# Three attention phases of a decoder: heads' values taken for two chunks in a row, and a new opening

## The chip, the cores and the metric

The kernel runs on one NeuronCore of a Trainium2 chip. The metric is the device time of one execution in microseconds (us), lower is better. Times are given as the median of several executions; the profile comes from one execution of its own.

## The reference

Two transformer layers on x of 16 batches (B), 256 tokens (S) and 512 features (C), with 16 heads of width 32:

```python
x = layer0_cross_attention(x, ctx, mask) + x      # pre-LN of x and ctx, softmax over 256 keys, output projection
x = x + fc2(gelu(fc1(LN(x))))
x = layer1_self_attention(x)                      # causal, LN after it
x = layer1_cross_attention(x, ctx)                # LN, relu feed forward, LN
```

Each attention computes q and k·v from features (512 wide products), scores q·k per head, a softmax over the keys, and the weighted sum of the values. A key row that is entirely zero is handled in layer 1 by a length ("energies" of one query against all keys decide where a row is cut). All is float32; a product is made of three passes on rounded parts (hi·hi, lo·hi, hi·lo), whose rounded halves are named `_hi` and `_lo`.

## The kernel before, in words

The program runs four phases after one another: **mask** (layer 0 cross attention), an MLP phase, **causal** (layer 1 self attention) and **cross** (layer 1 cross attention and feed forward). The change touches mask, causal and cross. They share `attention_phase`, with one program for each engine (SyncE, GpSimd = POOL, ScalarE = ACT, VectorE = DVE, TensorE = PE). A phase loops over the 16 batches. The heads of a batch are taken in four chunks (c = 0 to 3) of four heads. The order in which each engine issues its steps is written out by hand in `mask_turn`, `causal_turn` and `cross_turn`, for each engine its own; semaphores tie the engines together. Nothing reorders an engine's instructions: what stands behind a waiting instruction waits too. "Steady" batches are 1 to 15 in the loop; the first and last of a phase overlap the neighbouring phase or have no neighbour.

What happens to chunk c of batch b, by engine and line:

- `queries(b, c)` and `keys(b, c)` on PE (12 matmuls each, 256 columns, L172): q and k of four heads into one PSUM bank. ACT `qk` (L838 to 847) copies them rounded, DVE `qk_lo` (L1366 to 1371) makes the low halves. In causal and cross, POOL `query0` (L652) picks out a query, PE `energies0` (L2021) takes its product with all keys, and DVE `cuts` (L1374 to 1384) counts the kept keys (`flags`, L1379, signals `len_ready`) and writes the cut.
- `scores(b, c)` on PE (L2039, 24 matmuls on tiles of 32 rows by 128 columns; L2045 adds the cut).
- DVE minima (L1406 to 1412), then ACT `exps(b, u)` (L865, eight units' halves: u counts the heads, 4c to 4c+3), each followed by a read of its sum.
- `turn_probs(b, u)` on PE (L2060, four transposes, three in causal); ACT `copy(b, u)` (L877) takes them to `probT`.
- `attend(b, c)` on PE (L2079, 16 matmuls on tiles of 128 rows by 32 columns) into the left half of bank O; ACT `attended` (L885, L887) copies it to `OT`; PE `attended` (L2088, two transposes) turns it into the right half of O; DVE `attended` (L1432 to 1436: reciprocal, product, z) or, in mask, `turn_sums` (L2096, two transposes of the sums on PE) and DVE `normed` finish it. `attend` of chunk c stands behind `scores` of chunk c+1 (chunk 3 behind chunk 0 of the next batch).
- Between these steps PE does the `values` (L172), in mask `project`, in cross `feed1`, `feed2` and `post_turn`.

Order on PE around one chunk of the mask loop:

```python
turn_sums(b, 0)
scores(b, 1)
attend(b, 0)
queries(b, 2); keys(b, 2)
turn_probs(b, 4); turn_probs(b, 5); turn_probs(b, 6)
project(b, 0, 0); project(b, 0, 1)
turn_probs(b, 7)
```

The opening of the program: SyncE issues the loads of x and ctx of batch 0 (L391, L393), then `load_vecs` (L457 to 463; `where_vecs` L358 gives 16 small strided copies of the four layer norm vectors into `wcol`, columns of feature scales), then the weight matrices (L455), the mask (L443) and the rest. Then ACT `matrix_hi` (L815 to 818), DVE `matrix_lo` (L1264 to 1267) and `turned` (ACT L821 to 828; DVE L1351 to 1359, which for batch 0 also makes the high halves, L1357) prepare the first products; ACT normalizes x in L1197 ahead of them.

## Time and profile before

| | |
|---|---|
| median of 3 runs | 2745.2 us (2743.96 to 2746.96) |
| profiled execution | 2744.09 us, span 2742.4 us |
| granted TensorE clock | 0.995 of full speed |
| PE busy | 2672.3 us, 97% |
| DVE, ACT, POOL busy | 71%, 57%, 27% |
| mask phase, a steady batch | 39.31 us |
| causal phase, a steady batch | 33.25 us |
| cross phase, a steady batch | 49.27 us |

The span is the time from the first to the last recorded instruction; the execution's own time is 1.7 us longer. "PE busy" counts matmuls that overlap each other, so a small idle share doesn't mean that the engine works at its best rate. A steady batch is taken from the start of its first scores to that of the next batch's.

### The profile page before, as it was taken

The numbers are of one execution on the slowest core, as the hardware profiler recorded it, in microseconds if no ns is written. First come the engines' busy times: TensorE is split into PE (matmuls) and PEld (weight loads), VectorE is DVE, ScalarE is ACT, GpSimd is POOL, SyncE is SP. The second block draws the span as 40 slices with busy tenths as digits, with TensorE's granted clock in tenths as the row PEclk, the third lists the DMA queues.
The fourth block names the chain that finished last, engine by engine and source line by source line (L and its number), as shares of the span: only waits on it lengthen the run. The fifth ranks groups of instructions, "written<-read, shape, count | busy, mean of one in ns | idle before, by whom it ended". The sixth has DMA issues, their size and how long they took to land.

```text
span 2742.4 us, 68931 instructions
## 1 busy us (share of the span) xinstructions
PE 2672.3 (97%) x24032; PEld 2329.0 (85%) x24032; DVE 1952.7 (71%) x5572; ACT 1558.8 (57%) x4829; POOL 734.9 (27%) x935
## 2 busy tenths in 40 slices
PE   5999999999999999999999999999899999999997
PEld 5888888888888888888889999998788888888886
DVE  6878888887534443445388887887688888888876
ACT  5777777777211111111277777777676766767763
POOL 2333333330000000001013333333233434334343
PEclk9999999999999999999999999999999999999998
DMA  4333333342311211113021111112322212222110
GB/s 152 110 106 97 108 124 102 100 143 86 92 59 34 61 46 46 46 46 100 24 78 46 46 46 46 48 53 73 108 67 69 87 61 75 78 66 95 61 52 19
DMA packets 182230, 202.57 MB, mean 74 GB/s; under 512 B 19344, under 2 KB 109456, under 8 KB 181264
## 3 DMA queue, kind: packets, MB, share of 16 engines
q1 hardware_dynamic: 182160, 201.66, 23.3%
q8 instruction: 41, 0.67, 0.1%
q14 instruction: 29, 0.24, 0.0%
HBM read 137.65 MB, written 63.96 MB: 74 GB/s over the span
## 4 chain that ended last, share of the span: by engine, by line
PE 82%; DVE 8%; ACT 5%; issue 3%; POOL 1%; DMA 1%; SPq 1%; DVEq 0%; ACTq 0%; POOLq 0%
PE mask_work L172 13%; PE mlp_f L3028 13%; PE mlp_acc L3046 13%; PE causal_work L172 9%; PE cross_work L172 9%; PE mask_attended L2079 2%; PE mask_scores L2039 2%; PE mask_probsT L2060 2%; PE mask_scores L2060 2%; PE causal_scores L2039 2%; ACT cross_prob L865 2%; PE cross_probsT L2060 2%; PE causal_attended L2079 2%; PE cross_scores L2039 2%; PE causal_probsT L2060 1%
## 5 line engine op out<-in xcount | busy, mean ns | idle before, releaser
L2824 ACT ACTIVATE mlp_h<-mlp_f,mlp_b1col 128x512 f32<-128x512 f32 x128 | 88.3, 690 | 524.3 <-PE mlp_f L3028 524.3
L3028 PE MATMUL mlp_f<-mlp_xT_hi,mlp_w 128*128 128x512 f32 x1024 | 335.4, 389 | 0.0
L2929 DVE CAST mlp_hT_hi<-mlp_h 128x512 fp32r<-128x512 f32 x128 | 58.2, 454 | 369.8 <-ACT mlp_h L2824 369.7
L3046 PE MATMUL mlp_acc<-mlp_w,mlp_hT_hi 128*128 128x512 f32 x1024 | 315.2, 389 | 0.0
L865 ACT ACTIVATE mask_prob<-mask_scores,mask_low 128x256 f32<-128x256 f32 x512 | 237.7, 485 | 93.5 <-DVE mask_low L1412 93.4
L865 ACT ACTIVATE causal_prob<-causal_scores,causal_low 128x128 f32<-128x128 f32 (+1 forms) x512 | 211.0, 432 | 87.6 <-DVE causal_low L1412 87.6
L865 ACT ACTIVATE cross_prob<-cross_scores,cross_low 128x256 f32<-128x256 f32 x512 | 237.4, 497 | 33.2 <-DVE cross_low L1406 26.1
L1412 DVE CUSTOM_DVE_ANT_0 mask_scores<-mask_scores,mask_mask 128x256 f32<-128x256 f32 x512 | 198.9, 461 | 50.9 <-PE mask_scores L2039 50.3
L3028 PEld LDWEIGHTS mlp_f<-mlp_xT_hi,mlp_w 128*128 128x128 f32 x1024 | 192.1, 188 | 40.6 <-DVE mlp_xT_lo L2915 0.4
L3046 PEld LDWEIGHTS mlp_acc<-mlp_w,mlp_hT_hi 128*128 128x128 f32 x1024 | 192.2, 188 | 39.8
L172 PE MATMUL causal_work<-causal_xT_hi,causal_w 128*128 128x256 f32 x1008 | 221.8, 293 | 1.1 <-DVE causal_qk_parts L1371 1.1
L3028 PE MATMUL mlp_f<-mlp_xT_lo,mlp_w 128*128 128x512 f32 x512 | 199.2, 389 | 0.0
L3046 PE MATMUL mlp_acc<-mlp_w,mlp_hT_lo 128*128 128x512 f32 x512 | 199.2, 389 | 0.0
L1412 DVE CUSTOM_DVE_ANT_0 causal_scores<-causal_scores,causal_tri 128x128 f32<-128x128 f32 (+1 forms) x512 | 164.5, 394 | 25.3 <-PE causal_scores L2045 24.0
L172 PEld LDWEIGHTS causal_work<-causal_xT_hi,causal_w 128*128 128x128 f32 x1008 | 168.6, 189 | 13.2 <-issue 11.7
L652 POOL TENSOR_SCALAR causal_q<-all_own_head,causal_qk_parts 128x128 fp32r<-128x128 f32 x128 | 52.7, 423 | 431.7 <-DVE causal_qk_parts L1371 421.0
L1406 DVE TENSOR_REDUCE cross_low<-cross_scores 128x2 f32<-128x512 f32 x256 | 159.9, 681 | 5.0 <-issue 3.4
L652 POOL TENSOR_SCALAR cross_q<-all_own_head,cross_qk_parts 128x128 fp32r<-128x128 f32 x128 | 60.2, 482 | 369.3 <-DVE cross_qk_parts L1371 356.0
L2790 POOL TENSOR_TENSOR mlp_y<-mlp_x,mlp_b2r 128x512 f32<-128x512 f32 x32 | 45.3, 1447 | 398.5 <-DVE all_rows_largest L2945 363.5
L172 PE MATMUL causal_work<-causal_xT_lo,causal_w 128*128 128x256 f32 x504 | 142.0, 282 | 0.0
L877 ACT ACTIVATE mask_probT<-mask_probsT 128x512 f32<-128x512 f32 x128 | 80.6, 630 | 75.1 <-PE mask_probsT L2060 75.1
L865 ACT ACTIVATION_READ_ACCUMULATOR cross_prob<-cross_scores,cross_low 128x1 f32 x512 | 117.7, 230 | 0.0
(349 smaller groups left out, 8236.2 us busy)
## 6 DMA issues: line engine op xcount, KB each, us to landing
cross_x_in<-after_attention SPq DMA_DIRECT2D x17, 512.0 KB, 4.1
mask_x_in<-in_x SPq DMA_DIRECT2D x16, 512.0 KB, 4.5
mask_c_in<-in_ctx SPq DMA_DIRECT2D x16, 512.0 KB, 5.3
mask_res<-in_x SPq DMA_DIRECT2D x16, 512.0 KB, 3.7
after_attention<-mask_res SPq DMA_DIRECT2D x16, 512.0 KB, 2.8
mlp_x<-after_attention SPq DMA_DIRECT2D x8, 1024.0 KB, 5.5
mlp_stage<-in_L_xattn_fc_w SPq DMA_DIRECT2D x8, 1024.0 KB, 5.6
after_layer<-mlp_y SPq DMA_DIRECT2D x8, 1024.0 KB, 4.3
```

Of the source, the lines that this page charges most:

```text
L172: last = pe.matmul(out, lhs(k, a), rhs(k, c), start=(k == 0 and n == 0), stop=(k == KC - 1 and n == len(PASSES) - 1))
L652: ins = pool.tensor_scalar(Q0[:, part, :], own_head[:], QK[:, c % 2, 1 - part, 0:1].bitcast(F32), 1.0, ALU.mult, ALU.mult)
L865: ins = act.activation(prob[:, u % 4, qt, 0:w], SC[h][:, FROM[qt]:FROM[qt] + w], ACT.Exp, bias=low[:, u % 4, qt:qt + 1], scale=-1.0, accum ...
L877: act.activation(probT[:, u % 8, 0:n], PT_BANK[u % HC][:, 0:n], ACT.Copy).then_inc(s["copied"], 1)
L1406: ins = dve.tensor_reduce(low[:, u % 4, :], SC[h][:].rearrange("p (t k) -> p t k", t=TT), AX_X, ALU.min)
L1412: ins = dve.tensor_tensor_reduce(SC[h][:, at], SC[h][:, at], extra, 1.0, F32_MAX, ALU.add, ALU.min, low[:, u % 4, qt:qt + 1])
L2039: ins = pe.matmul(SC[h][:, at], QK[own, r, 1 - a, qt * P:(qt + 1) * P], QK[own, r, 2 + p, 0:WIDTH[qt]], start=(m == 0), stop=(masked_ctx a ...
L2060: ins = pe.transpose(PT_BANK[h][:, at:at + P], prob[:, u % 4, qt, kt * P:(kt + 1) * P], ident[:])
L2079: ins = pe.matmul(O[h * DH:(h + 1) * DH, q0:S], V[:, kt, HC * (c % KC) + h, :], probT[:, (HC * c + h) % 8, kt * S:kt * S + S - q0], start= ...
L2824: act.activation(h32[:, m % 2, :], F1[m % 2][:], ACT.Gelu, bias=b1col[:, m:m + 1]).then_inc(s["gelu"], 1)
L3028: ins = pe.matmul(F1[m % 2][:], W[2 * (m // 4)][:, a, k, m % 4 * P:(m % 4 + 1) * P], xT[p][:, k, :], start=(k == 0 and n == 0), stop=(k == ...
L3046: ins = pe.matmul(ACC[t][:], hT[a][:, m % 2, t * P:(t + 1) * P], W[2 * (m // 4) + 1][:, p, m % 4, :], start=(m == 0 and n == 0), stop=(m = ...
```

## The change

All three attention phases now take the values of two chunks in a row. `attend(b, 0, 2)` stands behind `scores(b, 2)` and `attend(b, -2, 2)` behind `scores(b, 0)` of the next batch (in cross the first of them stands after the first half of `feed1(b, 0)`, ahead of `turn_probs(b, 8)`), so chunks 1 and 3 hold no `attend`. Bank O holds both chunks, and the transposes overwrite it in place. `OT`, `sums`, `rs` and `rs32` are doubled; ACT copies both chunks back to back (one copy in mask), DVE's steps run once for a pair on 512 columns, `turn_sums` once with four transposes. `flags` is dropped: its step writes into `cut`.

The opening of mask takes the layer norm vectors as they lie, with four contiguous copies (`wraw`), and 16 matmuls by slices of the identity and one DVE copy make `wcol`. The third matrix is loaded ahead of the mask; the matrix halves and turned parts are done in another order; the high halves of batch 0 go from DVE to POOL.

Further moves: in cross, `turn_probs(b, -1)` comes ahead of `scores(b, 0)`, `turn_probs(b, 3)` and `turn_probs(b, 11)` ahead of the scores behind them, `queries(b+1, 1)` ahead of `energies0(b+1, 0)`, and ACT's copies 11, 14 and 2 ahead of `relu`, `qk` and `values`. In causal, `energies0` of chunks 2 and 0 come ahead of `turn_probs(b, 4)` and `turn_probs(b, 12)`. In mask, `keys(b+1, 0)` comes ahead of `turn_probs(b, 12)`.

```diff
     def where_vecs():
         if masked_ctx:
-            return [(wcol[q * QUAD:(q + 1) * QUAD, i, :],
-                     v.rearrange("(i k) q -> i k q", i=QUAD)[:, :, q:q + 1].rearrange("i k o -> i (k o)"))
-                    for i, v in enumerate(vecs[0:4]) for q in range(QUADS)]
+            return [(wraw[:, i, :], v) for i, v in enumerate(vecs[0:4])]
...
             load_vecs()
             load_matrix(0)
             load_matrix(1)
+            load_matrix(2)
             load_mask(0, first=True)
-            load_matrix(2)
...
+            for k in range(NP):
+                turned_hi(0, k)
             constants()
...
-            matrix_hi(0)
-            act.wait_ge(s["vec_loaded"], IT * NV)
+            matrix_hi(0, (0, 1))
+            act.wait_ge(s["columns_ready"], 1)
             turned(0, 0)
             turned(0, 1)
-            matrix_hi(1)
+            matrix_hi(0, (2, 3))
             turned(0, 2)
             turned(0, 3)
+            matrix_hi(1)
...
+            pe.wait_ge(s["vec_loaded"], IT * NV)
+            for k in range(KC):
+                for q in range(QUADS):
+                    ins = pe.matmul(PT[q * QUAD:(q + 1) * QUAD, 4 * k:4 * k + 4],
+                                    ident[:].rearrange("p (i k) -> p k i", k=KC)[:, k], wraw[:, :, q],
+                                    start=True, stop=True)
+            ins.then_inc(s["columns_ps"], 1)
...
-        def attend(b, c):
-
-            pe.wait_ge(s["copied"], UNITS * b + HC * (c + 1))
-            if c in (0, 2):
-                pe.wait_ge(s["v_ready"], 2 * b + 1 + c // 2)
+        def attend(b, c, n=1):
+
             pe.wait_ge(s["z_done"], KC * b + c + 1)
...
+            for c in range(c, c + n):
+                pe.wait_ge(s["copied"], UNITS * b + HC * (c + 1))
+                if c % 2 == 0:
+                    pe.wait_ge(s["v_ready"], 2 * b + 1 + c // 2)
+                at = S * (c % 2)
+                for kt in range(TT):
+                    q0 = P if causal and kt else 0
+                    for h in range(HC):
+                        ins = pe.matmul(O[h * DH:(h + 1) * DH, at + q0:at + S], V[:, kt, HC * (c % KC) + h, :],
+                                        probT[:, (HC * c + h) % 8, kt * S:kt * S + S - q0],
+                                        start=(kt == 0), stop=(kt == 1))
+                ins.then_inc(s["av_done"], 1)
+
+        def attended(b, c, n=1):
+
+            pe.wait_ge(s["ot_done"], KC * b + c + n)
+            for i in range(n):
+                for qt in range(TT):
+                    at = S * (c % 2) + (n * qt + i) * P
+                    ins = pe.transpose(O[:, at:at + P], OT[(c + i) % 2][:, qt * P:(qt + 1) * P], ident[:])
+            ins.then_inc(s["z_ps"], n)
```

The orders on PE, one phase each:

```diff
         def mask_turn(b, prev, cur, nxt):
...
-            turn_sums(b, 0)
             scores(b, 1)
-            attend(b, 0)
             pe.wait_ge(s["qk_lo"], KC * b + 2)
             queries(b, 2)
             keys(b, 2)
...
-            turn_sums(b, 1)
             if not nxt:
                 yield ROOM
             scores(b, 2)
-            attend(b, 1)
+            attend(b, 0, 2)
...
             turn_probs(b, 9)
+            turn_sums(b, 0)
...
         def causal_turn(b, prev, cur, nxt):
...
             scores(b, 1)
-            attend(b, 0)
...
             queries(b, 3)
+            energies0(b, 2)
             turn_probs(b, 4)
-            energies0(b, 2)
             keys(b, 3, 0)
             turn_probs(b, 5)
-            attended(b, 0)
...
             scores(b, 2)
-            attend(b, 1)
+            attend(b, 0, 2)
...
             scores(b, 3)
-            attend(b, 2)
...
         def cross_turn(b, prev, cur, nxt):
...
+                turn_probs(b, 2)
+                values(b, 0, 1)
+                turn_probs(b, 3)
 
             if cur:
                 scores(b, 1)
-                turn_probs(b, 3)
                 pe.wait_ge(s["qk_lo"], KC * b + 3)
                 queries(b, 3)
-
-            if cur:
-                if not prev:
-                    pe.wait_ge(last["z_done"], KC * B + 1)
-                attend(b, 0)
                 keys(b, 3)
                 turn_probs(b, 4)
...
             if nxt:
-                energies0(b + 1, 0)
                 pe.wait_ge(s["qk_lo"], KC * (b + 1) + 1)
                 queries(b + 1, 1)
+                energies0(b + 1, 0)
```

## Rows read from the trace of the kernel before

**Rows 1.** The page: busy time of each engine, and the chain by engine

```profile
PE 2672.3 (97%) x24032; PEld 2329.0 (85%) x24032; DVE 1952.7 (71%) x5572; ACT 1558.8 (57%) x4829; POOL 734.9 (27%) x935
...
PE 82%; DVE 8%; ACT 5%; issue 3%; POOL 1%; DMA 1%; SPq 1%; DVEq 0%; ACTq 0%; POOLq 0%
```

**Rows 2.** Windows of one steady batch each: stretch, length, busy PE, PEld, DVE, ACT, POOL

```profile
269.09:308.40 39.31, 39.27 (x402) 34.38 (x401) 31.86 (x104) 28.41 (x93) 13.87 (x19) 1.00 0.36 109
1512.13:1545.38 33.25, 33.25 (x404) 30.24 (x405) 26.96 (x115) 25.52 (x92) 10.38 (x16) 1.00 0.15 47
2120.14:2169.41 49.27, 49.00 (x501) 43.49 (x501) 42.21 (x95) 33.19 (x103) 18.87 (x22) 1.00 0.24 75
```

**Rows 3.** Timeline of PE, mask chunks 1 and 3: start, us, line, operation, count

```profile
278.91 0.98 PE L2039 MATMUL mask_scores<-mask_qk_parts 32*128 32x256 f32 x24
...
280.83 0.39 PE L172 MATMUL mask_work<-mask_xT_hi,mask_w 128*128 128x256 f32 x1
...
283.80 1.03 PE L2060 MATMUL mask_scores<-all_ident,mask_prob 128*128 128x128 f32 x8
284.67 0.60 PE L2060 MATMUL mask_probsT<-all_ident,mask_prob 128*128 128x128 f32 x4
...
301.77 1.29 PE L2060 MATMUL mask_scores<-all_ident,mask_prob 128*128 128x128 f32 x8
```

**Rows 4.** Timeline of ACT, mask chunk 1: end of the third unit's exponentials

```profile
283.62 0.22 ACT L865 ACTIVATION_READ_ACCUMULATOR mask_prob<-mask_scores,mask_low 128x1 f32 x1
```

**Rows 5.** Timeline of PE, causal chunks 2 and 3

```profile
1528.65 0.56 PE L2039 MATMUL causal_scores<-causal_qk_parts 32*128 32x128 f32 x12
...
1529.78 0.86 PE L2079 MATMUL causal_attended<-causal_probT,causal_v 128*32 128x256 f32 x16
1530.57 0.39 PE L172 MATMUL causal_work<-causal_xT_hi,causal_w 128*128 128x256 f32 x1
...
1534.61 0.44 PE L2088 MATMUL causal_attended<-all_ident,causal_ot 128*128 128x128 f32 x2
...
1537.09 0.56 PE L2039 MATMUL causal_scores<-causal_qk_parts 32*128 32x128 f32 x12
```

**Rows 6.** Timeline of DVE, causal chunk 2

```profile
1535.52 0.42 DVE L1436 TENSOR_TENSOR causal_z<-causal_attended,causal_rs 128x256 f32<-128x256 f32 x1
1535.86 1.27 DVE L1473 BATCH_NORM_STATS2 causal_stats<-causal_res 128x6 f32<-128x512 f32 x2
...
1537.71 0.69 DVE L1371 TENSOR_TENSOR causal_qk_parts<-causal_work,causal_qk_parts 128x512 fp32r<-128x512 f32 x1
```

**Rows 7.** Timeline of PE, then ACT, then DVE, cross chunk 1

```profile
2130.69 0.63 PE L2039 MATMUL cross_scores<-cross_qk_parts 32*128 32x256 f32 x12
...
2139.28 0.60 PE L2060 MATMUL cross_probsT<-all_ident,cross_prob 128*128 128x128 f32 x4
...
2133.03 0.47 ACT L865 ACTIVATE cross_prob<-cross_scores,cross_low 128x256 f32<-128x256 f32 x1
...
2136.98 0.65 ACT L847 ACTIVATE cross_qk_parts<-cross_work 128x512 fp32r<-128x512 f32 x1
...
2138.27 0.41 DVE L1379 TENSOR_SCALAR_CACHE_REDUCE cross_flags<-cross_probsT 128x256 f32<-128x256 f32 x1
```

**Rows 8.** Waits of PE: time waited in total, times, longest

```profile
PE cross_probsT L2021 <- POOL cross_q L652: 5.6, 15, 1.9
```

**Rows 9.** The chain of the opening: start, us, what

```profile
11.55 0.60 SPq L459
...
12.19 5.17 DMA mask_probT<-in_L_xattn_q_w
...
31.42 0.91 PE mask_scores L2039 x23
```

**Rows 10.** Timeline of ACT, the opening, and of POOL, a pair of casts

```profile
7.49 1.52 ACT L1197 ACTIVATE mask_x_in<-mask_x_in,mask_first_bias,mask_rstd 128x512 f32<-128x512 f32 x2 [5.41 <-POOL mask_first_bias L772]
...
292.42 1.17 POOL L626 CAST mask_xT_hi<-mask_x_turned 128x512 fp32r<-128x512 f32 x2 [2.42 <-PE mask_work L172]
```

More of the change, by code:

```diff
@@ L621, in turned_hi @@
         def turned_hi(b, k):
-            if k % 2 == 0:
+            if k % 2 == 0 and not (isinstance(b, int) and b == 0):
                 pool.wait_ge(*((s["qk_ps"], KC * b) if k else (s["x_left"], b)))
@@ L1260, in vector @@
     def vector(dve):
-        head = {"mask": 8, "causal": 13, "cross": 14}[kind]
-        per = {"mask": 6, "causal": 17, "cross": 23}[kind]
+        head = {"mask": 6, "causal": 9, "cross": 10}[kind]
+        per = {"mask": 4, "causal": 13, "cross": 19}[kind]
         chain = Chain(dve, s["chain"], head, per)
@@ L1378, in cuts @@
             dve.wait_ge(s["e0_ps"], n)
-            dve.tensor_scalar(flags[:], PT[:, 0:S], 0.0, None, ALU.not_equal, ALU.add, accum_out=lens[:, one]
-                              ).then_inc(s["len_ready"], 1)
+            dve.tensor_scalar(cut[:, c % 2, :], PT[:, 0:S], 0.0, None, ALU.not_equal, ALU.add,
+                              accum_out=lens[:, one]).then_inc(s["len_ready"], 1)
             dve.wait_ge(s["len_ready"], n)
@@ L1761, in cross_turn @@
             if cur:
-                attended(b, 1)
+                attended(b, 0, 2)
+            if cur and prev:
+                minima(b, 3, (0, 1))
             if prev:
@@ L1769, in cross_turn @@
             if cur:
-                minima(b, 3)
+                minima(b, 3, (2, 3) if prev else range(HC))
             if nxt and after:
@@ L1777, in cross_turn @@
                 fed(b, 0)
-            if cur:
+            if cur and not nxt:
                 attended(b, 2)
@@ L2068, in turned_free @@
                 pe.wait_ge(s["copied"], UNITS * b + HC * c)
-        def attend(b, c):
-            pe.wait_ge(s["copied"], UNITS * b + HC * (c + 1))
-            if c in (0, 2):
-                pe.wait_ge(s["v_ready"], 2 * b + 1 + c // 2)
+        def attend(b, c, n=1):
             pe.wait_ge(s["z_done"], KC * b + c + 1)
-            for kt in range(TT):
-                q0 = P if causal and kt else 0
-                for h in range(HC):
-                    ins = pe.matmul(O[h * DH:(h + 1) * DH, q0:S], V[:, kt, HC * (c % KC) + h, :],
-                                    probT[:, (HC * c + h) % 8, kt * S:kt * S + S - q0],
-                                    start=(kt == 0), stop=(kt == 1))
-            ins.then_inc(s["av_done"], 1)
@@ L2191, in mask_end @@
         def mask_end(b):
-            turn_sums(b, -1)
-            attend(b, -1)
+            attend(b, -2, 2)
             yield ROOM
@@ L2270, in mask_turn @@
                 queries(b + 1, 0)
+                pe.wait_ge(s["t_lo"], NP * (b + 2))
+                keys(b + 1, 0)
             turn_probs(b, 12)
@@ L2301, in causal_turn @@
             if prev:
-                attend(b, -1)
+                attend(b, -2, 2)
             if not cur:
@@ L2376, in causal_turn @@
             scores(b, 3)
-            attend(b, 2)
             if nxt:
@@ L2400, in cross_turn @@
         def cross_turn(b, prev, cur, nxt):
-            if cur and prev:
-                scores(b, 0)
             if prev:
                 turn_probs(b, -1)
-            if cur and prev:
+                scores(b, 0)
+                attend(b, -2, 2)
                 pe.wait_ge(s["qk_lo"], KC * b + 2)
                 queries(b, 2)
-            if prev:
-                attend(b, -1)
-            if cur and prev:
                 keys(b, 2)
@@ L2483, in cross_turn @@
             if cur:
+                if not prev:
+                    pe.wait_ge(last["z_done"], KC * B + 1)
+                attend(b, 0, 2)
                 turn_probs(b, 8)
@@ L2514, in cross_turn @@
                 scores(b, 3)
-                turn_probs(b, 11)
+                if not nxt:
+                    attend(b, 2)
             if nxt:
@@ L2555, in cross_turn @@
                 turn_probs(b, 14)
+            if nxt:
+                keys(b + 1, 1)
         def turn(b, prev, cur, nxt):
```

230 lines of the change are left out of this document (107 added, 123 removed).

## The prediction, made blind

> **What bounds the kernel now.** The page first: PE is busy for 97% of the span, and the chain that ended last lies on PE for 82% of it [rows 1]. Then windows of one batch in the middle of each phase: PE is covered for 39.27 of 39.31 us, 33.25 of 33.25 and 49.00 of 49.27, DVE for 81 to 86% of each, ACT for 67 to 77% [rows 2]. So next to no idle PE time is left to win in steady batches. What can be won on PE is time in which it counts as busy and does not flow at its rate, and what can be lost is the slack of the other engines. Such time shows in the timeline, by starts. A transpose in a row of its kind takes .109 us (eight in 284.67 − 283.80 = .87), the 24 products of `queries` and `keys` 283.80 − 280.83 = 2.97, or .124 each. The scores take .91 [rows 3, 9]; attend is what is left between 278.91 and 280.83, 1.92 − .92 = 1.00 [rows 3]. Inside, its 16 matmuls run in four tiles side by side; four rounds at .215 us are .86, so .14 is the cost of getting in and out of that tile shape. Another .10 sits in the first products behind it (2.97 against 24 × .12). Last the opening: the chain runs through 16 issues on SyncE of .64 us each until 12.15, then the load of the first matrix, 5.17 us, and reaches the first scores at 31.42 [rows 9].
>
> **Opening.** Twelve of 16 issues go: the first matrix is issued 12 × .64 = 7.7 us earlier, at 4.5, and lands at 9.7 if the load still takes 5.17. ACT must have ended its rows of x, at 9.01 [rows 9, 10], so it doesn't hold this up. Behind it DVE and ACT work alternately until 31.42; the four high halves move from DVE (about .4 each) to POOL, at 1.17 for two [rows 10], where the lows of DVE wait for them and cover is matrix work. The 16 new matmuls, priced like transposes at .109, and a copy of some .2 are 2 us ahead of the turned parts; they need the four small loads alone, and PE is idle then, waiting for ACT's rows of x until 9.01, so I cost them at nothing; without that cover they would be 2 us. The new order asks for half of matrix 0 ahead of the first turned parts, which lets them start earlier. I take −8.0. Bounds: −6, if the load is slower since it now meets the loads of x and ctx, and POOL's casts stand on the way; −9.5 with all casts won. Batch 0 of mask, bound by ACT, adds −1 (0 to −2).
>
> **Mask, a batch of 39.31 us.** Gone: one entry and exit of attend per pair, 2 × .14 = .28; a wait at `turn_probs(b, 13)`, whose eight transposes take 1.29 against 1.03, about .20 of the .26 [rows 3], since `keys(b+1, 0)` now covers it; .07 of transposes between shapes. Without new waits that is 38.76. But attend leaves chunks 1 and 3, while the exponentials keep their distance from the scores: they follow scores, minima and eight halves at .45. The third unit ends at 283.84, 4.93 behind the scores' start [rows 3, 4]. PE now comes to `turn_probs(b, 6)` at .92 + 2.97 + .87 = 4.76, and the result is seen at about 5.00: .245 lost. The same at `turn_probs(b, 14)`. So 39.25, or **−.05 a batch, −.7 in 14**. In chunks 0 and 2 attend grows by .86, so their exponentials have more time, and the rest of PE's work hides ACT's one 512 wide copy. Bounds: −.55 × 14 = −7.7 with both waits at nothing; +.4 × 14 = +5.6 if the exponentials come .2 later in both.
>
> **Causal, a batch of 33.25 us.** Attend is .79 (1529.78 to 1530.57) [rows 5], the pair 1.44: −.14 per pair, −.28, and −.10 for a hesitation at the turned values (transposes at 1534.61 behind OT) that gets cover. Against it the new wait that I hold most likely: DVE. The turned values stand 5.96 behind the scores of chunk 2; they move to about 6.55 (.65 of second attend less the hesitation). Two more transposes (.22) and DVE's z, started .91 behind them, 512 wide at about .61 in place of .34 [rows 5, 6], put the row statistics from 7.21 to about 8.30, +1.09. Behind these on DVE's queue stands `qk_lo(b+1, 0)`, at 1537.71, or 9.06 behind those scores [rows 5, 6]; it now starts at 10.15 and is seen at 10.85. PE wants it for `queries(b+1, 1)` at 8.44 + .65 + .22 − .10 + 1.12 = 10.33 (chunk length, second attend, two transposes, hesitation, the next scores). About .54 lost per batch. Chunk 1 without attend adds .14 at `turn_probs(b, 4)`, which waits for its exponentials, .10 at `queries(b, 3)` and .04 at `turn_probs(b, 7)`, together .82. Net **+.44 a batch, +6.4 in 14.5**. Bounds: −.38 × 14.5 = −5.5 with no new wait; +.9 × 14.5 = +13 if DVE's delay also moves the minima of chunk 3 behind it.
>
> **Cross, a batch of 49.27 us.** Gone: two entries and exits of attend, and switches at the transposes now ahead of the scores, together .76; the wait of `energies0` for POOL's query, 5.6 us in 15 waits [rows 8], .3 a batch in the records, .53 by the starts around it, since `queries(b+1, 1)` covers it. That gives 47.98. New: in chunk 1 attend and a turned probability are taken out, 1.8 us of the 8.59 ahead of `turn_probs` at 2139.28, so PE reaches `turn_probs(b, 6)` at 6.79 behind the scores. The other way around it waits for `len_ready`: exponentials from 2133.03, 2.34 behind the scores, come .34 earlier, OT's copy leaves ACT (.36), so ACT's `qk` starts at 5.59 and not 6.29, DVE's low half follows it, flags start at 6.88 (7.58 before) and are seen at 7.37 [rows 7]: .58 lost. Period 48.56: **−.7 a batch, −9.8 in 14**. Batch 0 of cross, where the longest of the POOL waits was 1.9 [rows 8], −2. Bounds: −1.3 × 14 = −18 with no wait; 0 if a second wait of the same size opens in chunk 3.
>
> The orders in each phase that I cost at nothing (ACT's copy 2 ahead of values, copy 11 ahead of `relu`, DVE's minima ahead of the hidden parts) are hidden by 23% or more of idle ACT time and 14% of idle DVE [rows 2]; without that cover each would cost one copy, .55 a batch.
>
> **Sum.** −8 − 1 − .7 + 6.4 − 9.8 − 2 = −15.1: 2744.1 becomes 2729 for a profiled execution; the median stands 1.1 above that, so 2730. About 0.2% (5.5 us) is what a measurement of this kernel can tell from no change.
>
> **Rivals.** *A, no new waits* (.15). Attend and turns flow, the other engines keep pace: −9 − 7.7 − 5.5 − 18 − 2 = −42, 2703. For it: DVE and ACT have idle time, and the waits that I found rest on a few tenths each. Against it: PE is ahead of the exponentials in chunks without attend by plain addition. The Trainium skill, TensorEngine Tiling (Array Packing), section Key Properties, says that a switch of the tiling mode drains TensorE, while another tile of the same mode does not. By that rule every pair saves a drain in and a drain out in all phases, and with nothing else counted the time would be A's; the .14 and .10 at attend's edges agree in size, and no row shows what a drain alone costs.
>
> *B, the opening's gain is lost* (.10): the matrix load takes part of the bandwidth of the x and ctx loads and is itself later, or ACT and DVE, which are alternately busy from then on, hold the first scores. Then 2.5 in place of 9 are won: 2737. For it: the load of 5.17 was timed behind those of x and ctx, not beside them [rows 9].
>
> *C, slower* (.10): the chain scores, minima, exponentials, transposes sets the length of the chunks without attend. There are two per batch, six over the phases, 84 in 14 batches. If it is later than I worked out by one more ScalarE step, .36 each, 84 × .36 = +30: −15 + 30, or 2760. It decides from .18 each: there the whole is no gain. For it: mask's PE is short by .245 there, causal's by .14, so no slack is left. Against it: those chunks lose the OT copy from ACT, which lies behind the third unit and gives the fourth .36.
>
> *D, the pair is no longer cheaper* (.05): if the second attend pays the full 1.00, the three phases lose .28 each, 14 × .84 = +12: 2742.
>
> The forecast has .60, 2718 to 2740. Faster by over 0.2%: forecast .58, A .15, B .07: .80. Within: .10. Slower: .10. The range is 2706 to 2744: part of A below and C above is left out.
>
> **What would show it.** In the changed profile: four issues on L459, ACT's first `matrix_hi` at about 9.7, first scores at 23.4; pairs of attend of 32 matmuls in 1.86 (causal 1.44). Mask's period 39.25 with short waits at the transposes of probabilities; causal's 33.8 and a PE wait on DVE's `qk_parts` ahead of `queries` of about .5; cross's 48.55, the wait on POOL's query gone, and one on DVE's flags in its place. Wrong: causal's period below 33.1 (DVE isn't late), cross's at 48.0 (A), or mask's above 39.8 (C); a first scores start later than 26 (B).

## The result, and the profile after

The changed kernel takes 2749.64 us in the median of 12 runs (2746.1 to 2755.6), the kernel before 2744.57 (2741.64 to 2746.96, 12 runs). The ratio is 1.0022, with a 95% interval of 1.0014 to 1.0030: slower by 5.1 us, where 15 us less were forecast. The profiled execution took 2750.05 us, its span is 2748.3 us.

The page of the changed kernel, busy time of the engines and the chain by engine:

```profile
PE 2670.9 (97%) x24064; PEld 2347.2 (85%) x24064; DVE 1897.8 (69%) x5284; ACT 1555.8 (57%) x4797; POOL 739.7 (27%) x939
...
PE 81%; DVE 7%; ACT 6%; issue 4%; DMA 1%; POOL 1%; SPq 0%; DVEq 0%; ACTq 0%; POOLq 0%
```

PE is busy for as long as before to .1% and DVE for 55 us less [rows 1]: neither tells that the kernel is slower. The windows do. One steady batch of each phase (mask, causal, cross), the columns as in [rows 2]; behind the engines' busy times stand the granted clock, the DMA share and GB/s:

```profile
266.87:306.32 39.45, 39.33 (x401) 34.55 (x400) 30.16 (x98) 28.19 (x90) 13.87 (x19) 1.00 0.34 108
1516.18:1550.17 33.99, 33.19 (x405) 30.58 (x404) 25.80 (x110) 25.36 (x92) 10.63 (x17) 1.00 0.14 46
2132.96:2181.72 48.76, 48.25 (x503) 43.61 (x502) 41.60 (x89) 33.39 (x103) 18.79 (x22) 1.00 0.23 75
```

In causal and cross the whole PE is now idle for .80 and .51 us of a batch, where it had been idle for 0 and .27. The waits of PE say where:

```profile
PE causal_work L172 <- DVE causal_qk_parts L1366: 11.4, 23, 1.5
PE cross_probsT L2059 <- DVE cross_cut L1374: 8.0, 16, 0.5
```

The wait on POOL's query in cross (5.6 us in 15) [rows 8] is gone. And the span from first scores to first scores, phase by phase, tells where the 5.9 us between the two profiled executions lie ("end of mask" and "end of causal" begin with the first scores of batch 15; the steady value for causal is the mean of 14 batches, 33.42, where the single window of [rows 2] has 33.25):

| stretch | before | after | difference | forecast |
|---|---|---|---|---|
| start to the first scores of mask | 31.35 | 25.42 | -5.9 | -8 |
| mask, batch 0 | 41.05 | 44.18 | +3.1 | -1 |
| mask, 14 steady batches | 39.31 each | 39.45 each | +1.9 | -.7 |
| end of mask and the MLP phase, to causal's first scores | 750.57 | 755.37 | +4.8 | 0 |
| causal, batch 0 | 38.34 | 36.94 | -1.4 | in the next row |
| causal, 14 steady batches | 33.42 each | 33.98 each | +7.9 | +6.4 |
| end of causal, to cross's first scores | 37.8 | 39.0 | +1.2 | 0 |
| cross, batch 0 | 55.0 | 57.7 | +2.7 | -2 |
| cross, 14 steady batches | 49.26 each | 48.77 each | -6.9 | -9.8 |
| end of cross | 80.4 | 79.0 | -1.4 | 0 |

The three loops together lose 2.9 us where a gain of 4.1 was forecast. The rest of the miss, 14 us, lies outside them: in the opening, the first batches and the ends.

There the granted clock differs, though the experiments will show that it isn't the whole of the matter. Three windows of the changed kernel, in batch 0 of mask (two) and of cross:

```profile
44.35:47.76 3.41, 3.41 (x40) 2.40 (x43) 2.25 (x8) 1.35 (x3) 0.00 (x0) 0.50 1.05 244
58.00:64.83 6.83, 5.63 (x25) 5.07 (x26) 4.87 (x16) 3.13 (x14) 1.93 (x4) 0.50 0.00 0
1955.81:1969.46 13.65, 12.87 (x76) 10.30 (x76) 4.69 (x10) 5.43 (x19) 3.75 (x3) 0.50 0.24 78
```

The column behind the engines' busy times is the clock: .50 of full speed, the lower of its two levels (1.2 and not 2.4 GHz). The kernel before had no such stretch in mask's loop at all, and two in cross's first batch (6.8 and 3.4 us). What PE did ahead of them shows in its timeline (start, duration, and in brackets the idle time before with what ended it), products of `queries`, `keys` and `values` left out:

```profile
41.36 0.63 PE L2059 MATMUL mask_probsT<-all_ident,mask_prob 128*128 128x128 f32 x4 [0.16 <-ACT mask_prob L866]
44.22 0.98 PE L2059 MATMUL mask_probsT<-all_ident,mask_prob 128*128 128x128 f32 x4 [2.23 <-ACT mask_probT L878]
45.12 1.66 PE L2038 MATMUL mask_scores<-mask_qk_parts 32*128 32x256 f32 x24
46.71 2.42 PE L2080 MATMUL mask_attended<-mask_probT,mask_v 128*32 128x256 f32 x32
...
58.45 2.02 PE L2059 MATMUL mask_scores<-all_ident,mask_prob 128*128 128x128 f32 x8 [2.19 <-ACT mask_prob L866]
```

PE stood for 2.23 and 2.19 us, and the clock fell .1 us behind the first of these and within the second. A wait of this length isn't always answered so: `dve_cross` (experiment 4), whose mask code is the same, kept its clock behind the first of them, and `order_cross` and `cross_pair`, whose mask code is that of the kernel before, had one fall of 3.4 us each in batch 0. Scores then take 1.66 us (.98 at the full clock [rows 3]), eight transposes 2.02 (1.03). The waits themselves are not much longer than the 1.85 to 1.87 us of the kernel before at the same kind of step; but chunks 1 and 3 of batch 0 now hold no attend, and they never held a projection.

### The profile page after: what moved, and what is told of

It reads as the page before. It is cut to its first block, busy times and chain, and to the rows that moved or that the text cites. A ratio compares the mean times of both kernels' runs of the same rounds, so it can differ in the third digit from the quotient of the medians.

```text
span 2748.3 us, 68472 instructions
## 1 busy us (share of the span) xinstructions
PE 2670.9 (97%) x24064; PEld 2347.2 (85%) x24064; DVE 1897.8 (69%) x5284; ACT 1555.8 (57%) x4797; POOL 739.7 (27%) x939
## 4 chain that ended last, share of the span: by engine, by line
PE 81%; DVE 7%; ACT 6%; issue 4%; DMA 1%; POOL 1%; SPq 0%; DVEq 0%; ACTq 0%; POOLq 0%
PE cross_work L172 13%; PE mlp_f L3022 13%; PE mlp_acc L3040 13%; PE mask_work L172 10%; PE causal_work L172 7%; ACT mask_prob L866 3%; PE cross_probsT L2059 2%; PE cross_attended L2080 2%; PE mask_probsT L2059 2%; PE mask_attended L2080 2%; PE mask_scores L2038 2%; PE cross_scores L2038 2%; ACT cross_prob L866 2%; PE cross_scores L2059 2%; PE causal_attended L2080 2%
## 5 line engine op out<-in xcount | busy, mean ns | idle before, releaser
L649 POOL TENSOR_SCALAR cross_q<-all_own_head,cross_qk_parts 128x128 fp32r<-128x128 f32 x128 | 47.3, 381 | 356.6 <-DVE cross_qk_parts L1366 343.5
L878 ACT ACTIVATE cross_probT<-cross_probsT 128x512 f32<-128x512 f32 x128 | 77.1, 602 | 107.7 <-PE cross_probsT L2059 107.5
```

Of the source, the lines that this page charges most:

```text
L649: ins = pool.tensor_scalar(Q0[:, part, :], own_head[:], QK[:, c % 2, 1 - part, 0:1].bitcast(F32), 1.0, ALU.mult, ALU.mult)
L878: act.activation(probT[:, u % 8, 0:n], PT_BANK[u % HC][:, 0:n], ACT.Copy).then_inc(s["copied"], 1)
```

## The experiments

Each was timed beside the kernel before on the same chip; the ratio is to that one. "The changed kernel" is the base unless another is named.

**1. Which part loses.** Four kernels made of the two versions of the attention code. `opening_alone` is the kernel before with the hunks of the opening. `mask_new` and `cross_new` take the new code for one phase (mask with its opening), and `causal_old` for all but causal. The edit of `causal_old` (the others are of the same kind):

```diff
-    phases.append(attention_phase(nc, "causal", x2, None, None, x3,
+    phases.append(attention_phase_before(nc, "causal", x2, None, None, x3,
```

> The kernel before with the new opening alone (wraw, 16 matmuls, matrix order, casts on POOL). Theory: the opening works about as forecast and its gain is real; first scores at 25.4 us as in the changed kernel (31.35 before), batch 0 of the mask phase back at about 41 us with no fall of the granted clock, total 5 to 6 us below the kernel before. Rival (the opening hands its gain back in batch 0, since ACT is late there): first scores at 25.4 but batch 0 at 44, total within 3 us of before.

> New mask phase and opening, causal and cross phases as before. From the two traces: opening -5.9, batch 0 +3.1, 14 batches +2, end of the phase and entry to the MLP +4.8, so +4 us in all (ratio 1.0015). If the losses around batch 0 and the end come from the neighbouring phases' new code, it would be -4 us.

> New cross phase alone. From the two traces: batch 0 +2.7, 14 batches -6.9, end -1.5, entry +1.2 at most: -4.5 to -6 us (ratio 0.998), with a steady batch of 48.76 (49.27 before). Rival: the cross phase gains only through what the causal phase leaves behind, then within 2 us of before.

> Mask and cross new, causal as before. From the two traces the causal phase costs 7 to 8 us (14 steady batches of 33.98 for 33.42, batch 0 -1.4, entry to cross up to +1.2): about 2742, 7.5 us below the changed kernel and 2 us below the kernel before. Rival: nothing of the loss is causal's own, then 2749.

| kernel | median us | before on that chip | ratio and interval |
|---|---|---|---|
| opening_alone | 2739.52 | 2743.73 | 0.9981 [0.9972, 0.9990] |
| mask_new | 2749.85 | 2743.73 | 1.0022 [1.0013, 1.0030] |
| cross_new | 2739.37 | 2743.73 | 0.9984 [0.9975, 0.9993] |
| causal_old | 2742.45 | 2743.73 | 0.9998 [0.9989, 1.0008] |

So the opening alone gains 4.2 us, and mask with it loses 6.1: **the new order of the mask loop (the pairs and the steps moved with them) costs about 10 us**, the largest single loss. Causal's part is +5.1 less -1.3, each against the kernel before on its own chip: 6.4 us. Cross gains 4.4. The sum, -4.2 + 10.3 + 6.4 - 4.4 = +8.1, stands above the measured +5.1; each kernel's ratio has an interval of some 2.5 us to both sides, so the parts add up no more closely than that. In `opening_alone` the first scores stand at 24.1 and batch 0 takes 42.6, so 1.5 of the 7.3 us won by then are handed back: less than in mask_new, where batch 0 took 45.7. That is neither the theory (41 and no fall of the clock; there was one of 3.4 us) nor the rival (44). With the same mask loop and an equal or nearly equal opening it took 41.5 to 42.6 in the profiles of `open_dve`, `open_warm` and the kernels of experiment 7, so a stretch of one execution is good to about 1 us here.

**2. The clock in the waits of batch 0.** Transposes of the identity that nobody reads, in the places of PE's waits in batch 0, the second of them also in the last batch; the attend bank O is free there:

```diff
             if prev:
                 ...
                 project(b, 0, 0)
                 project(b, 0, 1)
+            else:
+                filler(20)
             turn_probs(b, 7)
...
+            else:
+                pe.wait_ge(s["z_done"], KC * b + 3)
+                filler(18)
             turn_probs(b, 12)
```

> The changed kernel with idle transposes (20 and 18, of the identity, into the attend bank while it is free) in the waits of PE in batch 0 and in the last batch of the mask phase: ahead of turn_probs(b, 7) and ahead of turn_probs(b, 12). They compute nothing that is used. Theory clock: the waits of 2.2 to 2.5 us are what lets the granted TensorE clock fall to half for 3.4 to 6.8 us just behind them; with them filled, the clock stays whole from 28 to 1900 us, batch 0 goes from 44.2 to 40.4 and the end of the phase gains about 1 us: 4 to 5 us in all. Rival (ACT's chain is the length of batch 0, the clock is not on the path): batch 0 stays within 0.5 us of 44.2 and the total is the changed kernel's.

Measured: 2749.64, ratio 1.0017 [1.0008, 1.0026]. The profile shows the mechanism where it was put. The first two windows of above, and the end of the mask phase, in this kernel; a fourth for cross, where nothing was filled:

```profile
44.35:47.76 3.41, 3.41 (x62) 2.18 (x62) 3.27 (x12) 2.14 (x8) 0.00 (x0) 1.00 0.94 241
58.00:64.83 6.83, 5.36 (x45) 5.15 (x45) 4.71 (x12) 3.60 (x14) 0.84 (x2) 1.00 0.00 0
657.00:664.00 7.00, 6.65 (x58) 4.46 (x57) 2.78 (x7) 5.94 (x17) 0.00 (x0) 1.00 0.77 260
1955.50:1969.10 13.60, 12.82 (x75) 10.25 (x76) 4.80 (x10) 5.27 (x19) 3.85 (x3) 0.50 0.24 77
```

From 27 us on the clock stayed whole through the mask phase, batch 0 took 41.35 (44.18 without), and by causal's first scores the profiled execution stood 2.9 us ahead. But from there on it lost this again (end of causal 41.8 for 39.0, with two falls of 3.4 us each there for one), and the median of 11 runs shows no gain; the theory's 4 to 5 us in all fell. So the fall behind a wait is shown, and its cost in place; that a filler wins anything in the whole is not.

The end of the mask phase tells more. It took 754.55 us with the clock whole, 755.36 without the fillers and 750.57 before: of its +4.8 us the clock is .8, and 4.0 are something else. The last chunk's first transposes, in the kernel before and in the changed one, then two waits of PE in `warm_mask`:

```profile
657.39 0.66 PE L2060 MATMUL mask_scores<-all_ident,mask_prob 128*128 128x128 f32 x4 [1.19 <-ACT mask_prob L865]
...
658.00 0.66 PE L2059 MATMUL mask_scores<-all_ident,mask_prob 128*128 128x128 f32 x4 [2.18 <-ACT mask_prob L866]
...
670.69 0.74 PE L172 MATMUL mask_scores<-mask_w,mask_zT_hi 128*128 128x512 f32 x2 [0.86 <-DVE mask_zT_lo L1486]
674.27 0.73 PE L3050 MATMUL mlp_acc<-mlp_w,mlp_hT_hi 128*128 128x512 f32 x2 [0.53 <-DVE mlp_hT_lo L2935]
```

The transposes come 3.17 us behind the chunk's scores before and 3.16 in the changed kernel: the exponentials set this, and taking attend out ahead of them only lengthens the wait from 1.19 to 2.18. Of the 4.0 us 1.5 stand in the first three chunks of batch 15; the loop has 1.3 of these too and gets them back in chunk 3, this batch doesn't. Another 2.4 lie between the last scores and the MLP's first `mlp_acc` product (21.56 us behind them in `warm_mask`, 19.19 before): there the last two chunks are finished together, and the projection and the MLP wait 1.4 us for DVE, where PE had no such wait.

`warm_all` adds three groups of idle transposes in cross's batch 0 (20, 16 and 18); for the first of them the wait for the causal phase's last values comes ahead of `turn_probs(0, 3)`.

> The changed kernel with idle transposes in the waits of the mask phase's batch 0 and last batch, and also in the cross phase's batch 0: 20 ahead of turn_probs(0, 3), 16 ahead of scores(0, 2), 18 ahead of queries(1, 1). They compute nothing that is used. Theory clock: in the changed kernel chunk 2 of that batch takes 19.0 us since the clock is at half for 13.65 us of it (13.1 at a whole clock in the kernel with the new cross phase alone); filled, batch 0 of cross goes from 57.7 to 52 us and the total to 2741, 3 below the kernel before. Rival: the falls only move to other places, as in the run with the mask phase alone filled, and the total stays within 3 us of 2749.

Measured: 2749.03, ratio 1.0015 [1.0006, 1.0024]. Chunk 2 of cross's batch 0 is the cleanest view of the price. The same 143 matmuls in the changed kernel, and in `cross_new`, where the clock didn't fall at this place:

```profile
1954.46:1973.46 19.00, 18.22 (x143) 15.34 (x143) 7.62 (x15) 9.26 (x28) 5.11 (x4) 0.64 0.29 96
```

```profile
1945.90:1959.51 13.61, 12.32 (x143) 10.91 (x143) 8.09 (x16) 9.66 (x29) 5.64 (x4) 1.00 0.18 60
```

18.22 us of busy PE for the same matmuls against 12.32; what differs for them is the clock. With the fillers this chunk took 13.13 us. But the first of them, 20 at half clock with a wait for the causal phase's last values ahead, made chunk 0 longer (17.98 for 13.89), so batch 0 only fell to 55.1, and the median stayed. The spread shrank in this kernel, 4.6 us between the fastest and slowest of 11 runs against 9.5 of 12, but not in `warm_mask` (9.9).

This run also bears on what decides between faster and slower. Its granted clock was .994 to .997 over its runs, like that of the kernel before (.993 to .996) and not like the changed kernel's .988 to .992, and still it is 4.1 us slower than the kernel before. Its fillers cost about as much (the 4.1 us of chunk 0). So, as an estimate from these two numbers, a changed kernel with a whole clock and no price for it would be even with the kernel before, and not 15 us below it.

**3. Causal: DVE's order.**

```diff
             if prev:
                 row_stats()
-                ln_var(b, 0)
             if nxt:
                 qk_lo(b + 1, 0)
-            else:
+            if prev:
+                ln_var(b, 0)
+            if not nxt:
                 yield ROOM
```

> The changed kernel with DVE's low half of q and k of the next batch's chunk 0 taken between the row statistics and their sums (causal), ahead of ln_var instead of behind it. Theory: PE's wait ahead of queries(b+1, 1) of .61 us a batch is DVE's lateness; the low half comes .56 earlier, the wait falls to about .1, the period from 33.98 to 33.5, 6.5 to 7 us in all (2742.5). Rival: the wait goes elsewhere, to the minima of chunk 3 and from them to the transposes, and the period stays above 33.85.

Measured: 2747.46, ratio 1.0009 [1.0000, 1.0017]; a steady batch takes 33.86 (33.98). The step as it is in the changed kernel, PE and then DVE:

```profile
1544.01 0.38 PE L172 MATMUL causal_work<-causal_xT_hi,causal_w 128*128 128x256 f32 x1 [0.62 <-DVE causal_qk_parts L1366]
...
1541.41 1.28 DVE L1472 BATCH_NORM_STATS2 causal_stats<-causal_res 128x6 f32<-128x512 f32 x2
...
1543.27 0.68 DVE L1366 TENSOR_TENSOR causal_qk_parts<-causal_work,causal_qk_parts 128x512 fp32r<-128x512 f32 x1
```

and with the order changed:

```profile
1544.18 0.39 PE L172 MATMUL causal_work<-causal_xT_hi,causal_w 128*128 128x256 f32 x1 [0.28 <-DVE causal_qk_parts L1366]
...
1546.23 0.55 PE L2060 MATMUL causal_scores<-all_ident,causal_prob 128*128 128x128 f32 x3
```

The scores of chunk 3 start at 1542.20 and at 1542.72 in these two. The low half starts 1.07 us behind them in the one and .72 in the other, .35 earlier and not .56, and PE's wait is .34 shorter. The next transposes come 3.70 us behind the scores in the one and 3.51 in the other, so .19 are left: with the new order they wait for the exponentials (ended at 1546.18), whose minima now start 1.77 behind the scores and not 1.67. The chunk ends up .13 shorter, and .12 of a batch is won, not .5: DVE's low half did hold PE, and the next thing behind it is the chain scores, minima, exponentials. The theory had the first right and not the second, which was the rival's.

**4. Cross: what stands ahead of `len_ready`, and the moved query.**

```diff
-                qk_lo(b, 3)
                 cuts(b, 2)
+                qk_lo(b, 3)
```

> The changed kernel with DVE's cuts(b, 2) ahead of qk_lo(b, 3) in the cross phase. Theory: PE's wait at turn_probs(b, 6), .51 us a batch, is the count of the kept keys standing behind ACT's late copy of q and k; the count's own input is there 2 us earlier, so the wait goes to nothing, period 48.77 to 48.3, about 6.5 us in all. Rival: turn_probs(b, 6) then waits for its exponentials just as long (they end about .3 us earlier than the count), period at or above 48.6.

Measured: 2744.81, ratio 1.0000 [0.9991, 1.0008], 4.8 us under the changed kernel's median. Chunk 1 falls from 8.05 to 7.36 us and chunk 2 rises from 14.53 to 14.87; a batch takes 48.42. This is one of the 14 waits that opened (the page's sum for `cross_probsT` on ACT's copies is 8.7 us in 16 waits, 3.1 in 2 without the edit):

```profile
2247.23 0.63 PE L2059 MATMUL cross_probsT<-all_ident,cross_prob 128*128 128x128 f32 x4 [0.31 <-ACT cross_probT L878]
```

Half of what chunk 1 gained came back in chunk 2, where PE now waits for the copy of the transposed probabilities, whose bank it needs.

The other way around, the step that won: one step moved in the kernel before, and the same step put back in the new cross phase.

```diff
-                energies0(b + 1, 0)
                 pe.wait_ge(s["qk_lo"], KC * (b + 1) + 1)
                 queries(b + 1, 1)
+                energies0(b + 1, 0)
```

> The kernel before with one step moved: queries(b+1, 1) ahead of energies0(b+1, 0) in the cross phase. My step: PE's wait on POOL's query (5.6 us in 15 waits in the records, .53 a batch by the starts) goes. Steady cross batch 49.26 to 48.7 to 48.95, 4.5 to 7.5 us in all: then most of the new cross phase's gain (.50 a batch) is this order and not the pair. Rival: the pair carries it, and the period stays above 49.1.

> The new cross phase alone with one step put back: energies0(b+1, 0) ahead of queries(b+1, 1), as before the change. Theory: the order, not the pair, carries the new cross phase's gain, since the pair's gain (.14 to .28 a batch and the switches) is eaten by the .51 us wait for the cut. Period 49.1 to 49.3, total within 2 us of the kernel before. Rival: the pair carries it, period at or below 48.9.

Measured: `order_cross` 2738.63, ratio 0.9976 [0.9967, 0.9985]; `cross_pair` 2749.64, ratio 1.0022 [1.0013, 1.0031]. A steady batch of each:

```profile
2218.13:2266.85 48.72, 48.72 (x501) 43.45 (x500) 42.19 (x95) 33.23 (x103) 18.87 (x22) 1.00 0.24 75
```

```profile
2223.16:2272.72 49.56, 48.52 (x501) 43.65 (x500) 41.59 (x89) 33.38 (x103) 18.80 (x22) 1.00 0.24 74
```

48.72 with the order alone (49.26 before); 49.56 with everything of the change but this order. In `cross_pair` PE waits on POOL's query for 10.6 us in 15 waits:

```profile
PE cross_probsT L4518 <- POOL cross_q L3147: 10.6, 15, 3.2
```

The rival (the pair carries the gain) fell. The theory's cause stood but not its number, "within 2 us": without the moved query the new cross phase loses 5.5 us; with nothing but the moved query the kernel before gains 6.3. In the new cross phase the pair and its other moves add nothing to it (48.77 against 48.72) as long as the cut comes late, and .3 a batch when it comes early (48.42). Before the change PE had no wait on the cut, so the early cut only takes back a part of what the pair had opened.

**5. Mask: work ahead of the transposes that wait.**

```diff
+            if prev and nxt:
+                ...
+                project(b, 0, 0)
             turn_probs(b, 6)
...
+            if nxt and prev:
+                pe.wait_ge(s["proj_read"], TT * b + 1)
+                values(b + 1, 0, 0)
             turn_probs(b, 14)
```

> The changed kernel with half of project(b, 0) taken ahead of turn_probs(b, 6) and half of values(b+1, 0) ahead of turn_probs(b, 14) in steady mask batches. Theory: the two waits of about .32 us a batch at these transposes are the price of the chunks without attend; covered, the mask period falls from 39.45 to 38.85 (below the 39.31 of before), 8 us in all. Rival: the copies behind turn_probs(b, 7) come late instead, and the period stays above 39.3.

Measured: 2746.50, ratio 1.0003 [0.9994, 1.0012]. A steady batch:

```profile
266.51:305.74 39.23, 39.12 (x401) 34.50 (x401) 30.15 (x98) 28.24 (x90) 13.88 (x19) 1.00 0.34 109
```

39.19 in the mean of 14, .26 less than with the change as it is and .12 less than before; .60 had been forecast. Chunk 1 gained .27, chunk 3 nothing (8.94 for 8.88). There the moved values wait themselves, for a bank that DVE's sum must have read:

```profile
301.00 0.68 DVE L1495 TENSOR_TENSOR mask_res<-mask_work,mask_res 128x512 f32<-128x512 f32 x1
...
301.83 0.47 PE L172 MATMUL mask_work<-mask_w,mask_cT_hi 128*128 128x256 f32 x2
```

The values start 5.03 us behind the scores of that chunk, where the transposes had stood at 4.98. The rival's bound (above 39.3) was not met either.

**6. The opening.** Both on `opening_alone`: the four casts given back to DVE; and 5, 6 and 6 idle transposes ahead of the first queries, keys and values.

```diff
-            for k in range(NP):
-                turned_hi(0, k)
             constants()
...
+                if not squares(b):
+                    dve.wait_ge(s["t_act"], NP * b + k + 1)
+                    dve.tensor_copy(dst_t[0][:, sl, :], t32[k // 2][:, k % 2]).then_inc(s["t_hi"], 1)
```

> The new opening alone, with the high halves of batch 0 cast on DVE again and not on POOL. In the changed kernel DVE waited 1.15 and .51 us for POOL's casts and its own matrix steps took .69 to .85 us where they took .62; the four casts cost DVE 1.7. Theory: the casts on POOL gave nothing, first scores and total within .7 us of the new opening alone (first scores 24.1 to 25.8 by the clock's rise; total 2739.5). Rival (my prediction's step: moving them wins their 1.7 us): first scores about 1.7 later and 1.5 us more in all.

> The new opening alone, with 5, 6 and 6 idle transposes in PE's waits ahead of the first queries, keys and values. They compute nothing that is used. Theory clock: TensorE is granted half its clock until 21 to 27 us, which costs the first values and scores about 1.2 us where the rise comes late; with the gaps filled it rises earlier in most executions, total 1 to 2 us below the new opening alone. Rival: at half clock the idle transposes (.21 each) stand in the way of the first products, total the same or +1.

Measured: `open_dve` 2738.71, 0.9978 [0.9969, 0.9987]; `open_warm` 2737.32, 0.9977 [0.9968, 0.9986]; `opening_alone` had 0.9981. None of the three can be told from the others. In the changed kernel DVE waited for POOL's casts, and four of its matrix steps were longer beside POOL's constants, which the casts had pushed back to 16.10 to 18.95:

```profile
12.17 0.69 DVE L1354 TENSOR_TENSOR mask_xT_lo<-mask_x_turned,mask_xT_hi 128x512 fp32r<-128x512 f32 x1 [1.15 <-POOL mask_xT_hi L623]
13.37 0.69 DVE L1354 TENSOR_TENSOR mask_xT_lo<-mask_x_turned,mask_xT_hi 128x512 fp32r<-128x512 f32 x1 [0.51 <-POOL mask_xT_hi L623]
...
17.22 2.88 DVE L1265 SCALAR_TENSOR_TENSOR mask_w<-mask_probT,mask_w 128x512 fp32r<-128x512 f32 x4
```

while `open_dve` did the four casts itself and its last matrix step ended at the same time:

```profile
17.73 2.49 DVE L1269 SCALAR_TENSOR_TENSOR mask_w<-mask_probT,mask_w 128x512 fp32r<-128x512 f32 x4
20.14 2.49 DVE L1269 SCALAR_TENSOR_TENSOR mask_w<-mask_prob,mask_w 128x512 fp32r<-128x512 f32 x4
22.55 0.42 DVE L1394 TENSOR_SCALAR mask_mask<-mask_m_in 128x512 f32<-128x512 uint8 x1
```

(22.43 in the changed kernel). The casts on POOL bought .1 us.

**7. A version that beats both.** Mask and causal as before, the new opening, the new cross phase with the cuts first; then with idle transposes in cross's batch 0 (`best2`) and in the opening (`best3`):

> Mask and causal phases as before, the new opening, and the new cross phase with cuts(b, 2) ahead of qk_lo(b, 3). The parts alone gave -4.2 (opening) and -4.4 (cross); with the cut 6.5 more: -15 us, 2729. If the order of the cuts is worth nothing, 2735. If the gains of opening and cross were chance of the clock at the edges, above 2738.

> The best version so far (new opening, new cross phase with the cuts first, mask and causal as before: 2727) with the idle transposes in cross's batch 0. Theory clock: batch 0 of cross 52.9 to about 51.5, since less of it ran at half clock there; 1 to 2 us in all. Rival: nothing, or +1 from transposes that delay what stands behind them.

> Mask and causal as before, the new opening with idle transposes in its gaps, and the new cross phase with the cuts first. Without the idle transposes it was 2727.2 (17.6 below before). Theory: the clock's rise is earlier, 0 to 2 us more: 2725 to 2728. Rival: above 2729.

> The same kernel as best1, for more executions beside best3 on one chip: 2727 with an interval that excludes the kernel before; 0 to 2 us above best3.

| kernel | median us (runs) | before on that chip | ratio and interval |
|---|---|---|---|
| best1 | 2727.15 (5) | 2744.73 | 0.9932 [0.9919, 0.9946] |
| best1 again | 2727.74 (5) | 2744.61 | 0.9936 [0.9923, 0.9949] |
| best2 | 2727.64 (5) | 2744.91 | 0.9938 [0.9924, 0.9951] |
| best3 | 2724.84 (6) | 2744.61 | 0.9927 [0.9915, 0.9940] |

A steady batch of cross in `best1`:

```profile
2211.41:2259.84 48.43, 48.13 (x501) 43.60 (x501) 41.37 (x89) 33.45 (x103) 18.92 (x22) 1.00 0.24 76
```

17 us under the kernel before, 22 under the changed one. It isn't a part of the change alone: the cuts' order is one more step. By medians opening and cross gave 8.6, and the cuts' order .34 in each of 14 batches, 4.8; the whole is 4 us more than that sum. In the profiled executions nothing is left over: spans 7.5 (`opening_alone`) and 5.1 (`cross_new`) below the kernel before and 4.8 for the cuts are 17.4, and `best1` has 17.0. So the 4 us are of the size by which single executions and medians of these kernels differ. The idle transposes again give nothing that the intervals separate.

## Why the prediction was wrong

- **The pair's price** held: in steady batches a pair of attends took 1.86 us from start to the next step, 1.44 in causal. What a change of tile shape alone costs, no run shows.
- **Opening, "I take -8.0".** The first matrix did arrive early: ACT's first half of it started at 8.91, not 9.7. The step that failed is "work alternately until 31.42", taken as a fixed length behind the load: DVE's last matrix step ended 7.2 us earlier (22.5 for 29.7). A further 1.2 went since the values ahead of the first scores ran at half clock in the changed kernel (first scores at 25.42, against 24.08 in `opening_alone`). Alone, the opening is worth 4.2, between rival B's 2.5 and the least that I gave it, 6. "Batch 0 of mask adds -1" had the wrong sign: +1.5 in the opening alone, +3.1 in the whole.
- **Mask, "-.7 in 14".** The waits at `turn_probs(b, 6)` and `(b, 14)` came as worked out: transposes reached 282.63, and the third unit's exponentials ended 4.94 behind the scores. The loop is +.14 a batch and not -.05. The difference lies in chunks 0 and 1 (19.78 for 19.53); chunks 2 and 3 (19.68 for 19.79) came as forecast. Most of it is the turned sums: by the starts they cost .53 more in chunk 0 and save .45 at the ends of the two chunks, +.08, where the forecast had counted ".07 of transposes between shapes" as won. **The step that failed is the price of the ends: batch 0 at "-1", and no term at all for the end of the phase.** In batch 0 and in the last chunk there is no projection to fill the place of attend, and PE waits for ACT there with attend or without, so taking attend out wins next to nothing. Measured in place of -1 and 0: +3.1 and +4.8. Of the +3.1 the clock is 2.8 (41.35 with the fillers, still .3 over the 41.05 of before). Of the +4.8 it is .8; the other 4.0 stand with a whole clock: 1.5 that the last chunk doesn't give back and 2.4 behind its scores, 1.4 of them waits for DVE's part of the last pair and of the MLP. These two ends are 8.5 of the 13.2 us between the profiled executions of `mask_new` and `opening_alone`.
- **Causal, "+6.4 in 14.5".** Right in place and sign: the wait on DVE's low half ahead of `queries(b+1, 1)` was forecast at .54 and is .62, the period 33.8 and is 33.98. That the sum came out at 6.4 by `causal_old` and 6.5 in the trace is in part luck: the loop costs .56 a batch and not .44 (+7.9 in 14), and batch 0 gave 1.4 back.
- **Cross, "-9.8 in 14" and "batch 0, -2".** The wait for the cut, forecast .58 at `turn_probs(b, 6)`, is .51. The moved query is worth .53, as read from the starts and not from the list of waits. What was mis-sized is the .76 for entries and exits of attend and for switches: `order_cross` has 48.72 without the pair, and 48.72 + .51 - 48.77 leaves about .46 for it (the "-9.8" became -6.9). Batch 0 gained 2 on paper, since I took away POOL's wait of 1.9; the trace has +2.7, with 13.65 us at half clock behind a wait of 2.09. This one is the clock: with chunk 2 at the 13.1 us that it took at the full clock in `cross_new`, batch 0 would, as an estimate, be 3 us shorter than before.
- **The rivals.** A fell everywhere. C, chunks without attend set by the chain of the exponentials, was the mechanism that ended the causal experiment (3) and a part of mask's loss, but at .2 to .3 a chunk in some and not .36 in all; in batch 0 and the last chunk of mask it took away nearly all that attend's absence could win. D fell. None of the four had the granted clock. It took 2.8 us in mask's batch 0, .8 at its end and some 5.9 in cross's batch 0 in the profiled execution, but filling its waits moved no median, so that it decides between faster and slower is not shown.
- **The range** ended at 2744. It was built from the loops' unknowns; the ends of the phases had no term in it, and the first batches could only gain.

The Trainium skill, TensorE: Matmul & The Clock Gate, Part 1, says that the array's clock depends on how busy the array has lately been, and that the same kernel, at its start, gets the full clock at another matmul from run to run. The traces agree: half clock behind waits of about 2 us, though not behind every one, and in the 12 runs of the changed kernel, 9.5 us apart, the two slowest have a mean granted clock of .988 and .989 and the fastest .992.

Open: what the clock costs the whole kernel, since every filler that kept it was itself in the way or was followed by falls elsewhere, and what the pair is worth in mask and causal if the ends are left as before; that was not tried.

## What to carry to other kernels

Taking work out of a stage in which an engine just has enough moves the wait there, and in the first and last turn of a loop, where the filling work is missing, it opens one that the loop doesn't show: price the ends of a phase by themselves. A change with several parts should be timed in parts; here one moved query was worth more than the pairs, and the whole was 22 us slower than two of its parts with one more step moved. Where a wait is removed, look for what ends next .1 to .3 us behind it: in three of three cases a part of the forecast gain went there (.12 of .48 us a batch was won in causal, .26 of .60 in mask, .34 of .47 in cross).

## What the runs showed that was not expected

- PE stood for 2.1 to 2.3 us, and within or up to 1.4 us behind that the granted clock went to .50 for 3.4 to 13.7 us; the same 143 matmuls then took 18.22 us in place of 12.32. In `dve_cross` a wait of 2.23 us in mask's batch 0 had no such fall behind it.
- Idle transposes keep the clock whole in the stretch in which they stand (.50 to 1.00 in two windows), but the medians didn't move by more than the intervals.
- DVE's products of 128x512 took 2.88 us for four while POOL ran its constants (until 18.95), and 2.48 to 2.49 without that.
